# Token lists of 64 experts: counted and built by one-hot products instead of by sorted extraction; one program block; experts' weights loaded earlier

## The reference, cut to what matters

```
# per batch b (4 batches x 512 tokens x 512 channels)
x  = x + attention(norm(x), ctx) @ w_out.T
x  = x + swiglu_ffn(norm(x))        # width 1376, with 8 LoRA experts, top 2
x  = x + softmax(norm(similarity(norm(x), ctx)))
# over all 2048 tokens
h  = norm(x)
p  = softmax(h @ router_w.T)        # 64 experts
top 8 of p per token, their gates scaled to sum 1
for e in 64 experts:
    list(e) = the first 128 tokens, in order, that chose e   # capacity 128
    y = (silu(h[list] @ w_gate[e]) * (h[list] @ w_up[e]) * gate) @ w_down[e]
    x[list] += y
```

## Time and profile before

| | us |
|---|---|
| median of 3 runs | 1468.0 (1466.2 to 1468.45) |
| the profiled execution's own time | 1466.9 |
| its span in the trace | 1465.1 |
| attention(0) with the start, ffn(0) | 0 to 150, 150 to 268 |
| ffn(1), ffn(2), ffn(3) | 381 to 525, 640 to 775, 900 to 1020 |
| last tail | 1020 to 1073 |
| last list, then first gather | 1073 to 1103, 1103 to 1109 |
| experts, then the last additions | 1109 to 1430, 1430 to 1465 |

### The profile page before, as it was taken

How to read it: one execution, slowest core, us unless ns; L and a number is a source line. 1 busy time by engine, 2 the same in 40 slices (tenths; PEclk the granted TensorE clock), 3 DMA queues, 4 the chain that set the end, 5 groups by cost and what they waited for, 6 DMA issues and landing times. The chain is left out here.

```text
span 1465.1 us, 19951 instructions
## 1 busy us (share of the span) xinstructions
PE 1219.6 (83%) x6297; PEld 892.1 (61%) x6297; DVE 826.5 (56%) x1677; ACT 498.4 (34%) x1137; POOL 488.2 (33%) x539
## 2 busy tenths in 40 slices
PE   0698999887899987789998788998406999999990
PEld 0566777655777765567786566776204666666660
DVE  7674777576677758577866846664582222222220
ACT  1582312565222167422127633221202323333230
POOL 3530222633022372302236230121004555555541
PEclk9998999998999999999999989999757999999995
DMA  7002221000322100042200003220078999999966
GB/s 254 1 1 93 79 97 60 1 1 30 121 84 103 52 1 1 30 135 95 97 34 0 1 32 114 103 104 0 29 318 261 349 355 342 340 358 349 292 89 130
DMA packets 44659, 180.77 MB, mean 123 GB/s; under 512 B 5356, under 2 KB 8428, under 8 KB 35764
## 3 DMA queue, kind: packets, MB, share of 16 engines
q1 hardware_dynamic: 29732, 140.15, 25.5%
q0 software_dynamic: 14864, 39.85, 12.0%
HBM read 149.28 MB, written 34.90 MB: 126 GB/s over the span
## 5 line engine op out<-in xcount | busy, mean ns | idle before, releaser
L1819 PE MATMUL PS<-WE,XGT 128*128 128x384 f32 x512 | 194.8, 504 | 1.5 <-DVE HM L1929 0.8
L682 ACT ACTIVATE P<-PS,NM 128x512 f32<-128x512 f32 (+3 forms) x256 | 132.2, 536 | 50.7 <-DVE NM L1054 49.6
L1367 PE MATMUL PS<-XTH,WHI 128*128 128x512 f32 x352 | 141.6, 402 | 1.3 <-ACT SIL L825 1.3
L811 ACT ACTIVATE WHI<-WRAW 128x1280 fp32r<-128x1280 f32 x44 | 56.1, 1274 | 248.9 <-DMA WRAW<-in_ffn 248.9
L1368 PE MATMUL PS<-XTL,WHI 128*128 128x512 f32 x352 | 139.9, 397 | 0.0
L1369 PE MATMUL PS<-XTH,WLO 128*128 128x512 f32 x352 | 139.6, 397 | 0.0
L596 POOL CAST HH<-HID 128x512 fp32r<-128x512 f32 x44 | 28.1, 639 | 328.6 <-DVE HID L1279 317.1
L1232 DVE TENSOR_TENSOR WLO<-WRAW,WHI 128x584 fp32r<-128x584 f32 (+1 forms) x88 | 110.8, 1259 | 29.4 <-ACT WHI L811 17.3
L1054 DVE TENSOR_REDUCE NM<-PS 128x2 f32<-128x1024 f32 (+2 forms) x96 | 98.7, 1042 | 48.2 <-PE PS L1376 47.6
L1819 PEld LDWEIGHTS PS<-WE,XGT 128*128 128x128 f32 x512 | 88.2, 192 | 57.9 <-issue 23.5
L1427 PE MATMUL PS<-ident,P 128*128 128x128 f32 x640 | 101.6, 297 | 23.1 <-ACT P L682 12.8
(11 more groups left out here) (273 smaller groups left out, 2768.1 us busy)
## 6 DMA issues: line engine op xcount, KB each, us to landing
WE<-in_we SPq DMA_DIRECT2D x64, 1152.0 KB, 8.2
WRAW<-in_ffn SPq DMA_DIRECT2D x44, 932.0 KB, 4.6
hx<-HN SPq DMA_DIRECT2D x4, 1152.0 KB, 4.4
acc<-HN SPq DMA_DIRECT2D x17, 256.0 KB, 4.6
XIN<-in_x SPq DMA_DIRECT2D x4, 1024.0 KB, 10.5
out<-X SPq DMA_DIRECT2D x4, 1024.0 KB, 4.2
out<-acc POOLq DMA_DIRECT2D x1, 4096.0 KB, 23.0
CTX<-in_ctx SPq DMA_DIRECT2D x4, 256.0 KB, 7.5
```

The source lines that it names most:

```text
L682: act.activation(prob(t, n), PS[:, c0:c0 + (t + 1) * P], ACT.Exp, bias=NM[:, c:c + 1], accum_out=SSUM[:, c:c + 1]).then_inc(S["p_ready"], 1)
L811: act.activation(WHI[slot][:, 0:WD], WRAW[slot][:, 0:WD], ACT.Copy).then_inc(S["wg_hi"], 1)
L1367: pe.matmul(dst, a[0], b_[0], start=first, stop=False, **kw)
L1819: mm = pe.matmul(bank(2 + s % 2, 0, 2 * F1), XGT[s % 2][:, k, :], WE[s][:, k * 2 * F1:(k + 1) * 2 * F1], start=(k == 0), stop=(k == KC - 1))
```

## The change

The lists are built without sorting. Five small constants are loaded; `mk_ready` now releases PE's `positions`: products of the mask (now bf16) with a triangle of ones and with ones, which give each token's place in each expert's list; DVE adds what earlier batches took (TAKEN) and, for tokens that did not choose the expert, FAR = 1024. The place is split into a multiple of 8 and a rest. For each tile of 128 tokens DVE makes two one-hot arrays, HIGH (64 experts x 16) and LOW01 (64 x 8), multiplies the second with the token's number in its pair of tiles (LOW), and PE multiplies HIGH by LOW for eight experts at a time: 8 products of 128x64 into one bank. After two tiles DVE folds the bank into SLOTS. In ffn(b), b > 0, this is done for batch b-1: `positions` behind chunk 0 on PE, tiles behind chunks 2, 3, 6 and 7, the folds on DVE behind chunks 5 and 9. For batch 3, `last_list` does all four tiles in a row with separate buffers, ACT making the two scaled copies of each LOW, then a masked copy (OWN), eight products with SPREAD and two operations that give IDX.

There is one program block: the experts' buffers lie over buffers that are no longer used. The weights of experts 0 to 5 are loaded behind the chunk loads of ffn(3), those of 6 to 11 when its PE work is done. The rows of batch 3 are stored in two pieces. The ffn loops are written out. KEYS, LST, `list_round`, `keys`, the transposes of the mask and the reversed numbers go. The experts' own code stays as it was, with other function names.

```diff
@@ buffers
-    revt, KEYS, LST, next8, dummy
+    SLOTS = sb("SLOTS", [P, C]); TAKEN = sb("TAKEN", [P, E1]); AT = sb("AT", [P, NT, E1])
+    MK = sb("MK", [P, NT, E1], BF16)
+    HIGH = [sb(f"HIGH{i}", [P, E1, SA], BF16) for i in range(2)]
+    LOW = sb("LOW", [P, E1, SB], BF16)
+    LOW01 = sb("LOW01", [P, E1, SB], BF16)
+    LIST_TILES = (2, 3, 6, 7)
@@ SP, feed(b)
-                sp.wait_ge(S["key_ready"], 1 + b)
-                sp.dma_start(revt[:, :], w["revt"][:, cols(b, T)]).then_inc(S["rev_loaded"], 16)
+                for f in range(2, NF):
+                    load_w(f, f % 2)
+                    if last and f < 8:
+                        load_expert(f - 2, f - 2)
+                    if last and f == NF - 1:
+                        sp.wait_ge(S["tile_ps"], 1 + NT * (B - 1))
+                        sp.dma_start(SPREAD[:, :, :], w["spread"]).then_inc(spread_loaded, 16)
+                if last:
+                    sp.wait_ge(S["ffn_ps"], 1 + NT * B)
+                    for e in range(6, NW):
+                        load_expert(e, e)
@@ DVE, gates(b)
                 sig(dve.tensor_scalar(MK[:, :, :], SR[:, :, :], 0.0, None, ALU.is_lt), "mk_ready", b + 1)
+                step(dve.tensor_scalar(AT[:, :, :], SR[:, :, :], 0.0, FAR, ALU.is_ge, ALU.mult))
+                if b > 0:
+                    step(dve.tensor_tensor(AT[:, :, :], AT[:, :, :], TAKEN[:, :].unsqueeze(1).broadcast_to([P, NT, E1]),
+                                           ALU.add))
@@ DVE, the list
+            def positions(b, bk):
+                dve.wait_ge(S["pos_ps"], 1 + b + 1)
+                step(dve.tensor_tensor(whole, AT[:, :, :], bank(bk, 0, NT * E1)..., ALU.add))
+                ...                     # TAKEN <- totals, b < B - 1
+                step(dve.tensor_scalar(rest, whole, SB - 1, None, ALU.bitwise_and))
+                step(dve.tensor_scalar(whole, whole, ~(SB - 1) & 0xFFFF, None, ALU.bitwise_and))
+            def fold(b, q):
+                dve.wait_ge(S["tile_ps"], 1 + NT * b + 2 * q + 2)
+                ...                     # one copy, or three operations of 512 elements, then pair_out
+            def list_step(b, f):
+                if f == 1:
+                    dve.wait_ge(lists_loaded, 16 * len(LISTS))
+                    positions(b, 3)
+                if f - 2 in LIST_TILES and LIST_TILES.index(f - 2) % 2:
+                    fold(b, LIST_TILES.index(f - 2) // 2)
+                if f + 1 in LIST_TILES:
+                    t = LIST_TILES.index(f + 1)
+                    if t > 1:
+                        dve.wait_ge(S["tile_ps"], 1 + NT * b + t - 1)
+                    high(t, HIGH[t % 2]).then_inc(S["high_ready"], 1)
+                    step(low_01(t, LOW01))
+                    if t > 0:
+                        dve.wait_ge(S["tile_ps"], 1 + NT * b + t)
+                    dve.tensor_scalar(LOW[:, :, :], LOW01[:, :, :], numbers[:, 1 + t % 2:2 + t % 2], None,
+                                      ALU.mult).then_inc(S["low_ready"], 1)
+            def last_list():
+                positions(b, 6)
+                for t in range(NT):
+                    low_01(t, LOW4[0][t]).then_inc(S["low_01"], 1)
+                    high(t, HIGH4[t]).then_inc(S["high_ready"], 1)
+                dve.wait_ge(S["tile_ps"], 1 + NT * B)
+                ...                     # OWN <- bank 7 masked, own_ready
+                dve.wait_ge(S["list_ps"], 1 + 1)
+                ...                     # two operations of 64 elements: IDX, idx_ready
@@ DVE, ffn(b), two_chunks(i)
                     for d in (1, 2):
                         chunk(2 * i + d, d % 2)
-                        list_round(dve, (NF // 2 - 1) * 2 * b + 2 * i + d - 1, 2 * i + d - 1)
+                        if b > 0:
+                            list_step(b - 1, 2 * i + d)
                         if d == 2 and not last:
                             ...
                             front_q(b + 1, i)
@@ PE
+            def positions(b, bk):
+                pe.wait_ge(S["mk_ready"], 1 + b + 1)
+                for t in range(NT):
+                    for u in range(t + 1):
+                        mm = pe.matmul(bank(bk, t * E1, (t + 1) * E1), (before if u == t else ones)[:, :], MK[:, u, :],
+                                       start=(u == 0), stop=(u == t))
+                ...                     # four more for the totals, b < B - 1
+            def one_hots(bk, high, low, last):
+                for e in range(0, E1, GE):
+                    mm = pe.matmul(bank(bk, e * SB, (e + GE) * SB), high[:, e:e + GE, :]..., low[:, e:e + GE, :]...,
+                                   start=False, stop=last, skip_group_check=True)
+            def list_step(b, f):
+                if f == 0:
+                    positions(b, 3)
+                if f in LIST_TILES:
+                    t = LIST_TILES.index(f)
+                    ...                 # t == 0 and t == 2: wait for DVE, clear the bank
+                    pe.wait_ge(S["high_ready"], 1 + NT * b + t + 1)
+                    pe.wait_ge(S["low_ready"], 1 + NT * b + t + 1)
+                    one_hots(3, HIGH[t % 2], LOW, t % 2 == 1).then_inc(S["tile_ps"], 1)
@@ PE, ffn(b)
-                with pe.Fori(0, NF // 2) as i:
-                    for d in (1, 2):
-                        gate_up(2 * i + d, d % 2)
-                        down(2 * i + d - 1, (d + 1) % 2)
+                for f in range(NF - 1):
+                    gate_up(f + 1, (f + 1) % 2)
+                    down(f, f % 2)
+                    if b > 0:
+                        list_step(b - 1, f)
```

More of the change, by code:

```diff
@@ L110, in build @@
     zrow = sb("zrow", [1, 512], BF16)
[L111 to L115, removed]
     mhalf = sb("mhalf", [P, 8])
     IDX = sb("IDX", [P, E1], U32)
-    part3_base = place["at"]
+    before = sb("before", [P, P], BF16)
+    ones = sb("ones", [P, P], BF16)
+    steps_of = sb("steps_of", [P, SA + SB])
+    numbers = sb("numbers", [P, 3])
+    same = sb("same", [P, GE])
+    SLOTS = sb("SLOTS", [P, C])
+    TAKEN = sb("TAKEN", [P, E1])
+    AT = sb("AT", [P, NT, E1])
+    MK = sb("MK", [P, NT, E1], BF16)
+    lists_base = place["at"]
+    HIGH = [sb(f"HIGH{i}", [P, E1, SA], BF16) for i in range(2)]
+    tables_base = place["at"]
     cosw = sb("cosw", [P, NT, C])
@@ L273, in build @@
     acc_zeroed, combined = sem("acc_zeroed"), sem("combined")
+    lists_loaded, spread_loaded, idx_ready = sem("lists_loaded"), sem("spread_loaded"), sem("idx_ready")
+    expert_loaded = [sem(f"expert_loaded{s}") for s in range(NW)]
+    gathered = [sem(f"gathered{s}") for s in range(NX)]
+    LISTS = [(before, w["before"]), (ones, w["ones"]), (steps_of, w["steps_of"]), (numbers, w["numbers"]),
+             (same, w["same"])]
     tables_loaded, setup_loaded, setup_dve, setup_act, tables_made = (sem(n) for n in (
@@ L416, in ring, with experts, call @@
                     *(turned_by(ALONE, by) - turned_by(BESIDE, by) + turned_by(BESIDE, by) * a for by in "ad"))
+    def experts(engine, body, start, stop):
+        rounds = (stop - start) // NW
+        def call(i, d):
+            body((i * NW + start + d), (start + d) % NW, i + (start + d) // NW)
+        with engine.Fori(0, rounds) as i:
+            for d in range(NW):
+                call(i, d)
+        for e in range(start + rounds * NW, stop):
+            body(e, e % NW, e // NW)
     with nc.Block() as block:
@@ L615, in two_chunks @@
                         front_q(b + 1, i)
-                two_chunks(0)
-                alone(pool, "pool")
-                with pool.Fori(1, NF // 2 - 1) as i:
+                for i in range(NF // 2 - 1):
                     two_chunks(i)
@@ new lines, in _ @@
+            alone(pool, "pool")
+            experts(pool, expert, NX - AHEAD, E1 - AHEAD)
+            for e in range(E1 - AHEAD, E1):
+                scatter(e, e % NX, e // NX)
+            for parity in range(2):
+                pool.wait_ge(scattered[parity], 16 * (E1 // 2))
+            pool.dma_start(out[0:NTOK, :].rearrange("(a f) c -> a (f c)", f=NT),
+                           acc[0:NTOK, :].rearrange("(a f) c -> a (f c)", f=NT),
+                           accum_op=ALU.add, max_dma_last_dim=8192).then_inc(combined, 16)
@@ L841, in ffn @@
                 chunk(0, 0, b * N1 + 1)
-                with act.Fori(0, NF // 2 - 1) as i:
+                for i in range(NF // 2 - 1):
                     for d in (1, 2):
@@ L1303, in two_chunks @@
                             front_q(b + 1, i)
-                two_chunks(0)
-                alone(dve, "dve")
-                with dve.Fori(1, NF // 2 - 1) as i:
+                for i in range(NF // 2 - 1):
                     two_chunks(i)
                 chunk(NF - 2, 1)
+                if b > 0:
+                    list_step(b - 1, NF - 2)
                 if not last:
@@ L1689, in last_tail @@
                 mm.then_inc(S["lgt_ps"], 1)
[L1690 to L1694 removed]
+                last_list()
```

475 lines of the change are left out of this document (246 added, 229 removed).

## The result

The changed kernel takes **1494.0 us** (median of 4, 1493.1 to 1500.8) against 1467.1 for the kernel before in the same comparison: ratio 1.0196, 95% interval [1.0164, 1.0229], slower by 27 us. The forecast was 1496 (1472 to 1512). The profiled execution is the longest of the four, 1500.75 with a span of 1498.9; the spans of the other three are 1491.3 to 1492.7.

A forecast was written before the change was run, and what follows sets the result against it. PE bounds the ffns and experts, DVE the last list's gap. -20.7 + 1.9 + 11.1 + 25.6 + 11 = +28.9 us on 1466.9 gives 1496 us, slower; range 1472 to 1512.

The forecast's parts named there:

- last list, mask to IDX: Batch 3's list after the last router mask: IDX ready at 1082.4 instead of 1103.1, -20.7 us (bounds -24 and -15).
- operations ahead of LG: Gates on DVE in batches 1 to 3, for which PE waits: added operations cost +1.9 us (1.3 to 3).
- list products on PE: Ffns of batches 1 to 3: 46 products at 0.07 us plus two clears, 3.7 us each, +11.1 (5.6 to 17).
- waits on WLO: PE before gate_up(4) and its like at f=6: four waits of 5.3 us, two of 2.2, +25.6 (21 to 31.6).
- clock behind them: PE's clock after each of six stalls: 1.8 us more each, +11 us (0 to 16).
- experts: After IDX: gather, 7.5 us until PE starts and 64 experts stay unchanged, 0.
- The mechanism: Chunks 2 and 6: DVE idles some 12 us until PE frees LOW, then PE waits for DVE's LOW, front_q and WLO.
- The rival that DVE's spare time covers it: At f=2 and f=6 DVE finishes WLO before PE asks; stall and clock loss vanish: 1459 us; chance 0.12.
- The clock stays low: PE stays at 1.2 GHz about 13 us more around each of three ffns, losing 20 us: 1516; chance 0.08.
- written-out loops: Ffn loops: PE passes a loop edge at its usual 0.23 us a product, so writing them out gains 0.
- The prefetch: Last ffn: loading twelve experts' weights early saves 0, since PE never waited for them.

The follow-up runs named there:

- the best kernel: Two LOW buffers, AT made in the first list step and the rest of the last gates behind OWN, added to the changed kernel: 1458.0 us, ratio 0.9941 to before.

## Why the prediction was right, point by point

| term | forecast, us | measured, us | from |
|---|---|---|---|
| last list, mask to IDX | -20.7 | -19.9 | DVE's timelines of before and after |
| ahead of the last mask | none | -1.9 | the same; the clock of these executions |
| operations ahead of LG | +1.9 | +2.0 | attention stages; +2 back in the waits for LG when moved |
| list products on PE | +11.1 | +8.3 to +9.1 | two LOW buffers less no lists |
| waits on WLO | +25.6 | +20.8 | PE's waits |
| clock behind them | +11 | +8.6 | waits filled with products |
| around the waits | none | +1.1 | two LOW buffers (32.8), less 20.8, 8.6 and 2.3 |
| clock late behind LG | none | +7.9 | no lists in the ffns, against before (5.6), and the kernel after against two LOW buffers (2.3) |
| experts | 0 | -0.5 | windows |

The rows add up to 26.4 with 8.3 for the products.

**The mechanism was right.** The single LOW buffer makes DVE wait 11.6 us for PE (forecast some 12), and PE then waits for what DVE has left to do. Taking the cause away brings 30 us back. The rival that DVE's spare time covers it fell: DVE is idle 11.6 us at each place and PE waits all the same, because the release comes from PE itself.

**The waits** were sized a quarter too high: four are 4.2 us and not 5.3. WLO's first piece took 1.5 us (452.37 to 453.91), the time it has alone, and not 2.49. POOL's addition did run beside the pair, which took 3.25 us where it takes 2.29 with two LOW buffers and nothing beside it, but the delay fell on the second piece, for which PE doesn't wait there. LOW took 0.35 where I had 0.5. By the Trainium skill ("VectorE: DVE Perf Modes", The perf-mode tier table) my estimate was 0.3 for a bf16 tensor_scalar in SBUF; twelve took 0.352 to 0.355 us, so the trace agrees with it. The two of the last ffn were 1.9 each, forecast 2.2.

**The products** were sized too high: eight one-hot products take 0.41 us at the full clock, 0.05 each and not 0.07, and an ffn's 46 with their two clears cost 2.8 us and not 3.7.

**The last list** came out within 0.9 us (17.4 against 16.5) because two errors met. PE trailed DVE's last tile by 1.13 us and not 2.2. But OWN took 1.02 and not 0.69, and DVE waited 3.91 us for the products against SPREAD where I had 1.8 and a wait: they were scaled from fp32 rows at 0.115 us each and took 0.23. That was a misreading: the 32 products at 1057.55 us ran at a granted clock of 1.00, and the last list runs at 0.50, as the window of the old one had shown.

```profile
1057.50:1061.30 3.80, 3.73 (x34) 1.00 0.00 0
```

```profile
1133.10:1136.90 3.80, 3.65 (x16) 0.50 0.00 0
```

**The clock** was priced at 1.8 us at each of six waits. Four cost 1.6 to 2.7, the two short ones nothing: 8.6 in place of 11. Another 0.2 us was lost around each of the six.

**What no step had** is the clock's late return behind LG in ffn(2) and ffn(3), +7.9 us: 5.6 without any list step, and 2.3 more in the kernel after. The forecast had the clock fall only behind the waits; this is a part of what the rival *The clock stays low* describes: from LG to LDL of the three ffns the granted clock stood at 0.50 for 64 us in the kernel after and for 22 in the kernel before. With 8.6 and 7.9 the clock took 16.5 us in all, where the forecast had 11 and that rival 31.

I had priced the written-out loops at 0 and the trace at a loop's edge seemed to settle it. Written out, they cost 0.45 to 0.54% in the kernel before. The Trainium skill ("Runtime: NRT & Kernel Launch", Instruction fetch mechanics) prefers unrolling; here it gained nothing. The 6.3 us it lost there lie in the same two ffns as these 5.6, which makes the loops a likely cause. It isn't shown: with three engines' loops restored the best kernel was no faster, the absent transposes of the mask were not tested, and what the streams have to do with the clock stays open.

**The sum.** What was missed or too low (late clock 7.9, around the waits 1.1, last list 0.8) and what was too high (waits 4.8, products 2.8, clock 2.4, with 1.9 and 0.5 us gained outside of every step) nearly cancel: that 1496 met 1494 so closely is in part luck.

**The prefetch** at 0 is right against the kernel before and wrong as a statement of its worth. Before, 37 us of list hid the loads. With a list of 17 us they would stand ahead of the gather, and the trace without prefetch puts 4 us there. What a part is worth is to be asked in the kernel that the rest of the change leaves.

## What to carry to other kernels

A buffer that the busiest engine must release, written by an engine that the busiest one needs next, costs the whole work between the release and that need, however idle the writer is on average: look for the wait by order of instructions and not by busy shares, and pay for it with a second buffer (here 1 KB a partition, taken from a buffer that could be used in place, was worth 30 us).

A wait on TensorE costs its length and can cost more by the clock: here four waits of 4 us cost 1.6 to 2.7 more each, and a wait of 1.9 us cost nothing in some places and 1.6 in others. When comparing kernels to 0.5%, compare the stages, and see when the clock comes back in each.

## What was not expected of the hardware

- Without any change in PE's work or in its waits, the granted clock came back 5 or 12 us behind the same transposes, according to the kernel and the execution. This alone moved kernels by 3 us a stage, and no run here says what decides it.
- DVE's second LOW buffer is filled beside POOL's work on HID. There the same bf16 TENSOR_SCALAR takes 1.27 us instead of 0.35, six times in six, and the comparison ahead of it 1.10 instead of 0.69; POOL's cast took 1.53 instead of 0.61. It isn't the buffer's place: in the kernel after, the comparison writes the same place and takes 0.68 with no POOL work beside it and 1.10 (once 1.79) with it. The TENSOR_SCALAR has no such pair of rows. It costs nothing here, since DVE has the time. With two LOW buffers:

```profile
L1417 DVE TENSOR_SCALAR LOWB<-LOWB,numbers x6: 1268/1272/1275, 429.5 to 981.3; 128x512 bf16<-128x512 bf16 x6
...
L1417 DVE TENSOR_SCALAR LOW<-LOW,numbers x6: 352/354/355, 422.9 to 972.9; 128x512 bf16<-128x512 bf16 x6
```
